# Halved first loads, and quad 1's streams ahead of quad 0's rows, in a two-layer Winograd convolution kernel

## The reference

```python
# x: (16, 32, 48, 48) float32
def _gn(v, G=16, eps=1e-05):           # mean and variance over 2 channels x 48 x 48
    ...
    return ((g - m) / jnp.sqrt(s + eps)).reshape(v.shape)

# L0: 9x9 kernels, one rotated Gaussian for each (output, input) channel pair,
# made from (sx, sy, angle) and divided by its sum; zero padding 4; plus bias
# L1: dense 5x5 kernels, reflect padding 2 (written with an FFT)
x = x + _L0_conv_ref(_gn(x), L0_conv_weight, L0_conv_bias)
x = x + _L1_conv_ref(_gn(x), L1_conv_weight)
return x
```

## Time and profile before

| | us |
|---|---|
| median of 3 runs | 240.75 (240.49 to 240.94) |
| profiled execution | 241.09 |
| its span | 239.3 |
| PE busy | 232.4 (97%) |
| DVE busy | 211.6 (88%) |
| ACT busy | 157.8 (66%) |
| DMA, packets' share of 16 engines, SP's queue | 21.1% |

### The profile page before, as it was taken

One profiled execution on the slowest core, in us unless ns is written; L12 is line 12 of the kernel. 1 busy time (PEld: TensorE's weight loads), 2 busy tenths in 40 slices (PEclk: granted clock), 3 DMA queues, 4 the chain that ended last, 5 costly groups with the idle time before them and its releaser, 6 DMA issues.

```text
span 239.3 us, 4173 instructions
## 1 busy us (share of the span) xinstructions
PE 232.4 (97%) x1451; PEld 144.9 (61%) x1451; DVE 211.6 (88%) x460; ACT 157.8 (66%) x329; POOL 4.5 (2%) x12
## 2 busy tenths in 40 slices
PE   7999999999799999999999999999999999999995
PEld 7755656556466665556666665556666665555554
DVE  5989999898999999999989999999997459978943
ACT  6879899889489577999637694537459003569310
POOL 1000000230000000000000000000000000000000
PEclk9999999999999999999999999999999999999999
DMA  6980122320034000003422000162020002521123
GB/s 207 370 354 5 25 64 55 75 48 3 0 92 123 3 1 0 3 0 101 131 85 94 5 4 0 29 175 112 1 101 0 0 0 57 157 102 57 47 99 99
DMA packets 8709, 17.24 MB, mean 72 GB/s; under 512 B 3312, under 2 KB 5616, under 8 KB 8688
## 3 DMA queue, kind: packets, MB, share of 16 engines
q1 hardware_dynamic: 7712, 16.64, 21.1%
q10 hardware_dynamic: 976, 0.34, 0.6%
HBM read 5.57 MB, written 4.72 MB: 43 GB/s over the span
## 4 chain that ended last, share of the span: by engine, by line
PE 57%; DVE 26%; ACT 8%; issue 5%; DMA 3%; SPq 0%; DVEq 0%; ACTq 0%
PE banks L1508 29%; PE banks L1491 28%; DVE X L805 5%; DVE lo L772 3%; DMA X<-in_x 3%; ACT junk L1108 3%; DVE whl L565 2%; DVE wl L590 1%; ACT P L1141 1%; ACT hi L1164 1%; DVE work L560 1%; ACT arg L1188 1%; DVE arg L548 1%; ACT work L1206 1%; DVE X L812 1%
## 5 line engine op out<-in xcount | busy, mean ns | idle before, releaser
L1491 PE MATMUL banks<-hi,whl 128*128 128x360 f16 (+4 forms) x576 | 98.0, 318 | 2.2 <-ACT hi L1164 1.5
L1491 PEld LDWEIGHTS banks<-hi,whl 128*128 128x128 f16 x576 | 55.5, 98 | 36.7 <-issue 1.9
L1491 PE MATMUL banks<-lo,whl 128*128 128x376 f16 (+4 forms) x288 | 51.2, 318 | 0.0
L1108 ACT ACTIVATE junk<-X 128x576 bf16<-128x576 f32 x56 | 41.2, 737 | 2.8 <-DMA X<-in_x 0.8
L1491 PEld LDWEIGHTS banks<-lo,whl 128*128 128x128 f16 x288 | 27.9, 97 | 16.6
L1508 PE MATMUL banks<-hi,wh 128*128 128x384 f16 (+1 forms) x165 | 31.5, 320 | 0.2 <-ACT hi L1164 0.2
L1508 PE MATMUL banks<-lo,wh 128*128 128x384 f16 (+1 forms) x165 | 31.5, 320 | 0.0
L1508 PE MATMUL banks<-hi,wl 128*128 128x384 f16 (+1 forms) x165 | 31.5, 320 | 0.0
L1164 ACT CAST hi<-work 128x416 f16<-128x416 f32 x32 | 16.6, 536 | 16.9 <-PE banks L1508 11.9
L1154 ACT ACTIVATE work<-work,gof,gsc 128x26 f32<-128x26 f32 (+1 forms) x48 | 24.9, 609 | 3.6 <-DVE gof L666 3.6
L1164 ACT CAST hi<-s 128x384 f16<-128x384 f32 x32 | 15.4, 508 | 17.2 <-DVE s L739 10.9
(11 more groups left out here) (137 smaller groups left out, 233.4 us busy)
## 6 DMA issues: line engine op xcount, KB each, us to landing
X<-in_x SPq DMA_DIRECT2D x8, 576.0 KB, 10.1
out<-X SPq DMA_DIRECT2D x7, 576.0 KB, 2.8
work<-X SPq DMA_DIRECT2D x8, 432.0 KB, 3.8
whl<-work SPq DMA_DIRECT2D x24, 64.0 KB, 2.0
work<-X SPq DMA_DIRECT2D x8, 144.0 KB, 3.6
stage<-in_w SPq DMA_DIRECT2D x1, 640.0 KB, 8.0
work<-X SPq DMA_DIRECT2D x32, 12.0 KB, 2.3
out<-X SPq DMA_DIRECT2D x1, 384.0 KB, 2.6
```

The costliest lines, as they stand in the source:

```text
L1108: nc.scalar.activation(waste, image(n, m), function, accum_out=sums[c][:, col:col + 1]).then_inc(sums_done[c], 1)
L1491: ins = nc.tensor.matmul(dst[:, :, y0:y1], w[1][:, i, t * P:(t + 1) * P], src[:, :, y0 + IMG * dx:y1 + IMG * dx], start=(first and part == ...
```

## The change

- Pairs 0 and 1 are loaded in two halves each, with a semaphore for the first half (`x_half`); everything else that SP loads waits until pair 0 has landed, and the bias and layer 2's weights come last. The bias was issued by ACT before.
- PE warms up with 8 matmuls instead of 11, begins each plain sum on the first half, and takes two steps of the near rows ahead of the statistics' matmul.
- The weights of group 1 are scaled and cast in two parts of taps, as those of group 2 were.
- The last stream's mirrored weights are transferred in two parts, high and low.
- On DVE, quad 1's end streams stand ahead of quad 0's rows of group 1, and the wide ones 5 and 6 ahead of the rows of group 2; the low halves are placed between the two halves of a group's rows.
- On ACT, the casts of streams 5 and 6 and the bias read stand ahead of `channel_sums(2, 0, range(2))`; the casts of streams 3 and 4 stay behind it.
- In the second quad's list `middle1(1, 0)` comes first; layer 2's two weight sums read the contiguous copies that ACT made; layer 2's statistics stand ahead of half of the rows; its low weights are made one by one between the low halves. PE takes layer 2's statistics one stream later (k = 6 instead of 5).

```diff
+SPLIT = (1, 2)
-WARMING = 11
+WARMING = 8
...
+            def load_halves(n):
+                for at, landed in ((slice(0, PAIR // 2), x_half[n]), (slice(PAIR // 2, PAIR), x_loaded[n])):
+                    sp.dma_start(pair(n)[:, at], dram_pair(x, n)[:, at]).then_inc(landed, 16)
...
-            load(0)
-            load(1)
-            sp.dma_start(stage[:, :, :], w1).then_inc(stage_loaded, 16)
+            load_halves(0)
+            load_halves(1)
+            sp.wait_ge(x_loaded[0], 16)
             for n in range(2, NP):
                 load(n)
-            for at, i in enumerate(FIRST_ORDER):
+            sp.dma_start(bias_c[1][:, :], bias).then_inc(bias_loaded, 16)
+            sp.dma_start(stage[:, :, :], w1).then_inc(stage_loaded, 16)
...
+            for at, i in enumerate(FIRST_ORDER[:-1]):
                 if i not in TURN_BANKS:
                     turn(at, i)
+            turn_half(7, FIRST_ORDER[-1], 0, turned[LAST_TURNED])
+            turn_half(7, FIRST_ORDER[-1], 1, last_low_turned)
...
             def layer2_sums():
-                dve.wait_ge(stage_loaded, 16)
+                dve.wait_ge(ends2_ready, 2)
                 for i, op in ((1, ALU.add), (2, ALU.subtract)):
-                    tt(w2_at(i), block2(0), block2(1), op).then_inc(sums2_ready, 1)
+                    tt(flat2(g2t[:, i, :, :]), flat2(g2t[:, 0, :, :]), flat2(g2t[:, 3, :, :]), op).then_inc(sums2_ready, 1)
...
                 far1(1)
-                rows1(0, 1)
                 streams1_ends(1)
+                rows1(0, 1, (0,))
                 low_halves(1, 1, range(2, 4))
+                rows1(0, 1, (1,))
                 middle1(0, 2)
-                rows1(0, 2)
-                streams1_wide(1)
-                low_halves(1, 1, range(4, 8))
+                first_wide1(1)
+                second_wide1(1)
+                stream1(1, 5)
+                stream1(1, 6)
+                rows1(0, 2, (0,))
+                low_halves(1, 1, range(4, 6))
+                rows1(0, 2, (1,))
+                stream1(1, 3)
+                stream1(1, 4)
+                low_halves(1, 1, range(6, 8))
 
             def second_quad():
+                middle1(1, 0)
                 layer2_scale()
                 layer2_sums()
-                middle1(1, 0)
-                rows1(1, 0)
+                rows1(1, 0, (0,))
+                small_stats(2, 0)
+                rows1(1, 0, (1,))
                 end1(1, 2)
                 end1(1, 3)
-                small_stats(2, 0)
-                low_layer2()
+                low_layer2((0,))
                 streams2(0)
-                low_halves(2, 0, range(4))
+                low_half(2, 0, 0)
+                low_layer2((1,))
+                low_half(2, 0, 1)
...
             layer2_magnitude()
+            high_halves(1, 1, range(4, 6))
+            read_m1(1, 0)
             channel_sums(2, 0, range(2))
-            high_halves(1, 1, range(4, 8))
-            read_m1(1, 0)
+            high_halves(1, 1, range(6, 8))
             channel_sums(2, 0, range(2, 4))
...
-                pe.wait_ge(x_loaded[n], 16)
+                pe.wait_ge(x_half[n], 16)
...
+                    if k == steps // 2:
+                        pe.wait_ge(x_loaded[n], 16)
...
-            stats(1, 0)
             pe.wait_ge(identity_loaded, 16)
-            near_rows(1, range(6))
+            near_rows(1, range(2))
+            stats(1, 0)
+            near_rows(1, range(2, 6))
...
-                layer1(1, k, between=(2, 0) if k == 5 else None)
+                layer1(1, k, between=(2, 0) if k == 6 else None)
```

More of the change, by code:

```diff
@@ L124, in casts @@
     at = FIRST_ORDER.index(i)
-    return at + 1 + (1 if at >= FIRST_ORDER.index(2) else 0)
+    return at + 1 + sum(at >= FIRST_ORDER.index(j) for j in SPLIT)
 def order1(qd):
@@ L236, in build @@
         x_loaded = [sem(f"x_loaded{n}") for n in range(NP)]
+        x_half = [sem(f"x_half{n}") for n in range(2)]
         tab_loaded = sem("tab_loaded")
@@ L583, in layer2_scale, with low_layer2 @@
                 MARK["scale2"] = count[0]
-            def low_layer2():
+            def low_layer2(ks):
                 dve.wait_ge(sums2_ready, 2)
                 dve.wait_ge(ends2_ready, 2)
-                for k, i in enumerate(S2):
+                for k in ks:
+                    i = S2[k]
                     dve.wait_ge(wh2_done, k + 1)
@@ L796, in middle1, with rows1 @@
                 stt(pd[1][:, :], product1(qd, k), -f, mb[1][:, :], ALU.mult, ALU.add).then_inc(mid_done[1], 1)
-            def rows1(qd, g):
-                for which, src, factors in ((0, ps, EVEN_ROWS), (1, pd, ODD_ROWS)):
+            def rows1(qd, g, halves=(0, 1)):
+                for which in halves:
+                    src, factors = ((ps, EVEN_ROWS), (pd, ODD_ROWS))[which]
                     dve.wait_ge(mid_done[1], 6 * qd + 2 * g + which + 1)
@@ L890, in first_quad @@
                 dve.wait_ge(dve_w, MARK["krec"])
-                flat1 = slot(1).rearrange("p k (r o) -> p (k r) o", o=C)
-                done(stt(flat1, flat1, W_SCALE, krec[:, :].unsqueeze(1).to_broadcast([P, NT * RB, C]), ALU.mult, ALU.mult))
-                MARK["weights", 1] = count[0]
+                for half, taps in enumerate(STEPS2):
+                    at = slice(*taps)
+                    flat1 = slot(1)[:, at, :].rearrange("p k (r o) -> p (k r) o", o=C)
+                    done(stt(flat1, flat1, W_SCALE, krec[:, :].unsqueeze(1).to_broadcast([P, (taps[1] - taps[0]) * RB, C]), ALU.mult, ALU.mult))
+                    MARK["weights", 1, half] = count[0]
                 kernel_scale()
@@ L1192, in high_kernel, with high_kernel_parts @@
                 nc.scalar.copy(made_taps(wh, i), weight1(i)).then_inc(wh1_done, 1)
-            def high_kernel_two():
+            def high_kernel_parts(i):
                 for step, taps in enumerate(STEPS2):
                     at = slice(*taps)
-                    act.wait_ge(dve_w, MARK["weights", 2, step])
-                    nc.scalar.copy(made_taps(wh, 2)[:, at, :], slot(2)[:, at, :]).then_inc(wh1_done, 1)
+                    act.wait_ge(dve_w, MARK["weights", i, step])
+                    nc.scalar.copy(made_taps(wh, i)[:, at, :], slot(i)[:, at, :]).then_inc(wh1_done, 1)
             def turn_kernel(i, part):
@@ L1473, in conv1 @@
                     elif qd == 0 and first and part == 0:
-                        pe.wait_ge(wh1_done, casts(i) - (1 if i == 2 else 0))
+                        pe.wait_ge(wh1_done, casts(i) - (1 if i in SPLIT else 0))
                     elif qd == 0 and first and part == 2:
@@ L1484, in conv1 @@
                         pe.wait_ge(turned[i], 16 * RB)
+                    if qd == 0 and not first and part == 2 and i == LAST_TURNED:
+                        pe.wait_ge(last_low_turned, 16 * RB)
                     for t in taps:
-                        if qd == 0 and first and part == 0 and i == 2 and t == STEPS2[1][1] - 1:
-                            pe.wait_ge(wh1_done, casts(2))
+                        if qd == 0 and first and part == 0 and i in SPLIT and t == STEPS2[1][1] - 1:
+                            pe.wait_ge(wh1_done, casts(i))
                         dx = t - PAD1
@@ L1504, in conv2 @@
                         pe.wait_ge(lo_done[2], 4 * n + k + 1)
+                    if part == 2 and n == 0:
+                        pe.wait_ge(wl2_done, k + 1)
                     src = xbuf[2][:, i, :].rearrange("p (r y) -> p r y", y=ROW2)
```

22 lines of the change are left out of this document (17 added, 5 removed).

## The result

The changed kernel takes 243.22 us (median of 4 runs, 243.16 to 243.25); the kernel before took 240.84 beside it (4 runs, 240.49 to 241.04). The ratio is 1.010, with a 95% interval from 1.0083 to 1.0118: slower by 2.4 us. The forecast was 242.5, with a range of 241.7 to 243.5 and 0.80 for slower. The profiled execution took 243.25 us with a span of 241.4, against 241.09 and 239.3.

The account below looks back on a forecast made before the run. PE was taken as the bound, its start of pair 1 moving with DVE and ACT. DVE's ledger (+2.11, -1.20, +0.81, less 0.09, plus 0.07) gave +1.70 on 240.75: 242.45, rounded 242.5 us, range 241.7 to 243.5.

Parts of the forecast that it names:

- rival B: The start gives nothing because pair 1 lands at 8.16 or later; 243.1 us, chance 0.28.
- A: The forecast itself, 242.5 us, with its own range 241.8 to 243.0; chance 0.52.
- PE as the bound, and the ledger to its start of pair 1: PE is full after 100.05; DVE's lead or lag up to that start is added to the time.
- The start, -0.57: Loads to group 1's weights: pair 1 lands earlier, gaining 0.63 us, less 0.06 for one more DVE instruction.
- The turned weights: "that wait goes": PE's 0.40 us wait at 52.20 for the last stream's mirrored taps disappears with two-part transfer; alone it brings nothing.
- Streams ahead of rows: Quad 1's end streams: cast at 59.9, PE's 1.31 us wait at 63.91 gone, PE some 2.3 us ahead.
- Rows done, DVE's wait of 3.05, +2.11: Quad 0's rows end at 71.71; DVE waits 3.05 us at quad 1's last two low halves, ending 2.11 later.
- Rival D: DVE's wait at quad 1's last two low halves stays short, so the kernel is faster: 239.4 us, chance 0.13.
- Sums, -1.20: Layer 2's two weight sums on DVE take about 1.50 us from contiguous tiles instead of 2.70.
- The root, +0.81: Layer 2's statistics: the square root on ACT, due at 82.10, comes at 82.91 behind four scalings.
- Low weights +1.63, PE's start +1.70: Layer 2's low weights at 86.43 instead of 84.80; PE's start of pair 1 at 101.75 instead of 100.05.
- PE's lead ends in waits at pair 0 and here: PE's 2.3 us lead is lost at pair 0's first block (about 1 us) and at its start of pair 1.

Follow-up runs that it names:

- a1_start: Kernel before plus the new start only (halved loads, 8 warming matmuls, near rows ahead, split weights of group 1): 240.65 us, ratio 1.0003.
- c3_turn: Changed kernel with the last stream's mirrored weights transferred in one piece again: 243.18 us, ratio 1.0105.
- a2_ends: Kernel before with only quad 1's end streams moved ahead of quad 0's rows of group 1: 240.56 us, ratio 0.9999.
- c4_fill_only: Changed kernel with quad 1's middle step and layer 2's scale and weight sums moved ahead of the last two low halves on DVE: 242.4 us, ratio 1.0073.
- a3_wide: Changed kernel with wide streams, quad 0's last rows and the casts behind them back in the old order: 243.3 us, ratio 1.0111.
- c2_root: Changed kernel with the root of layer 2's statistics on ACT behind two of the four scalings instead of all four: 242.61 us, ratio 1.0082.
- b2_q2_back: Changed kernel with the second quad's list as before, contiguous weight sums and quad 1's changed order kept: 243.45 us, ratio 1.0132.
- a4_short: Changed kernel with layer 2's sums of quad 0's first two images taken over a quarter of each image: 241.67 us, ratio 1.0045.
- b5_fill: Changed kernel, DVE's wait filled, layer 2's statistics behind all rows, root ahead of the fourth scaling, three low weights ahead of pair 0's streams: 240.01 us, ratio 0.997.
- c1_fewer_waits: b5_fill without two DVE waits asked for twice, at the fourth low weight: 239.72 us, ratio 0.9962 to the kernel before.
- b3_sums: Kernel before with only layer 2's two weight sums reading the contiguous tiles: 240.17 us, ratio 0.9984.

## Why the prediction was right, and where it wasn't

The stated range held the result only because it took in rival B: A's own range ended at 243.0. In the traces the mechanism is A's all the same, and what brought the median above it is mainly one wrong reference and one small loss behind the start, both below.

- **PE as the bound, and the ledger to its start of pair 1.** Right. The start moved by +1.86 (forecast +1.70), and the time by this and by 0.27 more.
- **The start, -0.57.** In the two profiles -0.51 at the reciprocal and -0.44 where DVE comes to the moved end streams (58.47 against 58.91), less than the step's -0.57. Pair 1 was there when ACT came for it, as the step says; pair 0 was 0.28 later, which the step hadn't. But against the median it is worth nothing (a1_start). The step that failed is the reference: it took the landing in one execution for that of the kernel, and this execution was 0.48 above the later median. So the median came out at 243.2, near the number of case B (243.1), though B's condition, pair 1 landing at 8.16 or later, isn't what the trace shows. 1.86 + 0.27 + 0.48 = 2.61, which is 243.22 - 240.61.
- **Whether halves land earlier than a whole pair:** no run decides it. In the eleven kernels with halves ACT takes up pair 1 between 7.12 and 7.79 and never waits for it; with whole loads it waited once in three (until 8.16) and found it landed at 7.55 and 8.02. The time agrees with halves that bring nothing: a1_start, with them, took 240.65 us against 240.61.
- **The turned weights: "that wait goes".** Wrong. It moved from the high half to the low one and kept 0.32 us: the eight issues take 5.02 us on SP's queue, so the low half's last one is out at 51.6. The eight issues were counted, their 0.63 us each weren't. It cost nothing (c3_turn).
- **Streams ahead of rows.** Right: cast at 59.99 (forecast 59.9), PE's wait at 63.91 gone. And right that it brings nothing alone (a2_ends).
- **Rows done, DVE's wait of 3.05, +2.11.** 71.98 (71.71), 2.90, low halves from 75.78 (75.58). Right in place and size. What the ledger didn't say is that removing this wait gives back only 0.8 (c4_fill_only) or nothing (a3_wide). Rival D, in which the time falls with this wait down to 239.4, was thus priced wrongly: once 0.8 of the 2.90 us are gone, the next limits decide, the channel sums on PE and the root behind ACT's sums and scalings.
- **Sums, -1.20.** 1.56 us for two, -1.14.
- **The root, +0.81.** It came 0.99 behind the variance (82.09 to 83.08); in a1_start the root of quad 2's statistics comes 0.21 behind (92.20 to 92.41). So 0.78, and c2_root got 0.6 back. Right.
- **Low weights +1.63, PE's start +1.70.** +1.92 and +1.86. Of the 0.29 too little, 0.20 were there at the low halves already, 0.13 of them from the start.
- **PE's lead ends in waits at pair 0 and here.** At pair 0 1.23 and 0.37, at pair 1 0.79. The largest was not named: 1.61 at 98.49, where PE waits for ACT's reading of a bank of quad 1, which stands behind the normalising.
- **"Behind that PE is full".** Almost: 0.27 us by 169.58, from the gap on DVE at 124.8. In the trace before the same stall lies hidden under a wide operation (123.69 to 124.17), and the prediction doesn't count how the new list moves it.

## What to carry to other kernels

When a wait lies on the path, write down what the waiting engine would wait for next if it were gone: here, behind the wait at the low halves, stood two more limits within 0.8 us of it, the channel sums and the root. All three hang in part on one late event, quad 0's last row, and in part on their own place in a list: with the row early but PE's channel sums late (a3_wide), the time was the same. Work that fills the wait helps only together with the moves that shorten the chain behind it: filling gave 0.8 us, the root 0.6, both together with the statistics behind the rows and another order of the low weights 3.2. And before an early landing is credited, several executions should say how it scatters.

## What the runs showed of the chip

- After a wait of 3.28 us, PE's granted clock fell to 0.50 of full speed 1.3 us after PE had resumed, until about 84 us, and its matmuls took another 1.7 us (b2_q2_back); after the waits of 1.6 us in other kernels here it stayed at 1.00 (the longest 1.62, at 96.90 in a4_short). That the wait caused the fall is the author's inference from this one kernel.
- DVE's list stalls for some 0.35 us at quad 2's two wide operations in all fourteen kernels, each time behind the 318th or 319th record of DVE's list; what stalls it isn't shown. It costs DVE time only where no long operation is running to cover it (the changed kernel 0.35, b5_fill 0.36, c1_fewer_waits 0).
- PE's wait at 99.58 in a1_start was 0.16 us longer than the profile's idle time, 0.40 where it shows 0.24: with PE full a matmul is shown 0.32 us long, and the next one starts 0.16 behind its start (b3_sums).
